# Splitting six of the experts' second weight tiles early, with GpSimd making their low parts

## The reference

```
gi = x @ W_ih + b_ih ; gh = h @ W_hh + b_hh            # 256 steps in sequence, batch 16, width 512
r = sigmoid(i_r + h_r) ; z = sigmoid(i_z + h_z)
n = tanh(i_n + r * h_n) ; h = (1 - z) * n + z * h
combine = two largest of softmax((h / |h|) @ router_w), normalised
out = x + sum over 8 experts e of combine[e] * (h @ Wa[e] @ Wb[e])      # rank 128
```

## Time and profile before

| what | value |
|---|---|
| median of 3 runs | 1009.75 us |
| the profiled execution | 1010.27 us |
| its span | 1008.5 us |
| PE busy | 977.9 us (97%) |
| DVE busy | 878.0 us (87%) |
| ACT busy | 689.5 us (68%) |
| POOL busy | 292.9 us (29%) |
| chain that ended last | PE 91%, DVE 4%, DMA 2%, ACT 1% |

### The profile page before, as it was taken

How to read it: one execution, slowest core, us unless ns; L and a number is a source line. 1 busy time by engine, 2 the same in 40 slices (tenths; PEclk the granted TensorE clock), 3 DMA queues, 4 the chain that set the end, 5 groups by cost and what they waited for, 6 DMA issues and landing times.

```text
span 1008.5 us, 60534 instructions
## 1 busy us (share of the span) xinstructions
PE 977.9 (97%) x28939; PEld 668.9 (66%) x20799; DVE 878.0 (87%) x3637; ACT 689.5 (68%) x2696; POOL 292.9 (29%) x755
## 2 busy tenths in 40 slices
PE   4789999999999999999999999999999999999997
PEld 2456666666667666677666666666676676676674
DVE  6889888888888888888888888888888888888887
ACT  6687766776766676666677676677666667666664
POOL 1032323332323332323332332332233332233223
PEclk9999999999999999999999999999999999999999
DMA  8321111111111111111111111101111101110000
GB/s 298 93 81 31 28 33 31 27 30 32 29 31 33 28 27 35 27 31 33 29 25 35 28 32 29 33 23 35 30 30 30 32 22 35 31 30 20 14 9 29
DMA packets 49360, 38.83 MB, mean 39 GB/s; under 512 B 34532, under 2 KB 38972, under 8 KB 49084
## 3 DMA queue, kind: packets, MB, share of 16 engines
q1 hardware_dynamic: 48236, 31.41, 11.5%
q10 hardware_dynamic: 848, 3.54, 1.0%
HBM read 18.94 MB, written 8.39 MB: 27 GB/s over the span
## 4 chain that ended last, share of the span: by engine, by line
PE 91%; DVE 4%; DMA 2%; ACT 1%; issue 1%; SPq 0%; POOL 0%; DVEq 0%; POOLq 0%
PE pairs L882 17%; PE ybank L882 12%; PE gates L962 11%; PE gates L967 11%; PE pairs L873 8%; PE ybank L873 5%; PE zbank L882 5%; PE zbank L873 5%; PE obank L882 5%; PE nbank L882 5%; PE obank L873 3%; PE nbank L873 3%; DMA whh<-in_L_cond_W_hh 1%; DVE tr L747 1%; PE ybank L999 1%; DMA xin<-in_x 1%
## 5 line engine op out<-in xcount | busy, mean ns | idle before, releaser
L882 PE MATMUL pairs<-wx,xs 128*32 128x384 f16 x4096 | 281.4, 328 | 0.2 <-DVE wx L727 0.2
L609 ACT ACTIVATE rr<-pre 128x64 f32<-128x64 f32 x256 | 65.7, 257 | 245.8 <-DVE pre L750 245.8
L882 PE MATMUL ybank<-hparts,wa 128*128 128x128 f16 x2048 | 194.1, 219 | 0.0
L882 PEld LDWEIGHTS ybank<-hparts,wa 128*128 128x128 f16 x2048 | 159.9, 98 | 29.8 <-issue 16.7
L873 PE MATMUL ybank<-hparts,wa 128*128 128x128 f16 x1024 | 178.3, 219 | 0.0
L463 POOL TENSOR_TENSOR y<-y 128x128 f16<-128x128 f32 x256 | 106.2, 435 | 247.3 <-ACT y L660 241.8
L873 PE MATMUL pairs<-wx,xs 128*32 128x384 f16 x2048 | 174.6, 327 | 0.0
L882 PEld LDWEIGHTS pairs<-wx,xs 128*32 128x32 f16 x4096 | 108.5, 97 | 95.0 <-issue 55.3
L962 PE MATMUL gates<-whh,st 128*32 128x256 f16 x4080 | 157.3, 273 | 12.7 <-DVE st L776 12.2
L962 PEld LDWEIGHTS gates<-whh,st 128*32 128x32 f16 x4080 | 107.4, 96 | 76.8 <-ACT gates L581 47.1
L967 PE MATMUL gates<-whh,hparts 128*32 128x256 f16 x4080 | 157.1, 273 | 0.0
(11 more groups left out here) (137 smaller groups left out, 1803.1 us busy)
## 6 DMA issues: line engine op xcount, KB each, us to landing
out<-outb SPq DMA_DIRECT2D x63, 128.0 KB
xin<-in_x SPq DMA_DIRECT2D x58, 128.0 KB
wih<-in_L_cond_W_ih ACTq DMA_DIRECT2D x4, 768.0 KB, 7.8
whh<-in_L_cond_W_hh SPq DMA_DIRECT2D x4, 768.0 KB, 11.8
wih<-in_L_ffn_Wb SPq DMA_DIRECT2D x8, 256.0 KB, 2.7
xs<-xh SPq DMA_TRANSPOSE x116, 3.1
wih<-in_L_ffn_Wa SPq DMA_DIRECT2D x4, 256.0 KB, 5.2
whh<-in_L_ffn_Wa SPq DMA_DIRECT2D x4, 256.0 KB, 2.9
```

Of the source, the lines that this page charges most:

```text
L609: nc.scalar.activation(rr[:, :], pre[:, RG, :, :].rearrange("p k b -> p (k b)"), ACT.Sigmoid, scale=1 / PROD_SCALE).then_inc(r_ready, 1)
L882: return nc.tensor.matmul(out, lhsT, rhs, start=start, stop=stop, skip_group_check=True)
```

## The change

Wb's tiles of experts 2 to 7 leave the list SPLITS (SHARED = 2 keeps experts 0 and 1 in it). Their high part is made by ACT in steps 4 to 9 (high_wb, WB_AT = 4), behind the late split of the same step. Their low part is made by POOL, at the head of its beside(n) in the same steps: the float32 tile is multiplied by 128 in place, then the high part is subtracted in two halves of 256 columns. PE waits on a new semaphore for them. The order of the late loads changes (the list LATE), and SP issues two a step from step 2 on, so that each of the six tiles is asked for two or three steps before its high part is due. DVE keeps the splits of wb 0 and 1 in steps 10 and 11 and has none after that.

```diff
+    SHARED, WB_AT = 2, 4
...
-        for e in range(NE):
+        for e in range(SHARED):
             split_wb(e)
...
+        LATE = [("wa", i) for i in range(K)]
+        for i in range(NE - SHARED):
+            LATE += [("wb", SHARED + i)] + ([("wa", K + i)] if i < K else [])
+        LATE += [("wb", i) for i in range(SHARED)]
...
+            def late_at(n):
+                return range(LEAD + n, LEAD + n + 1) if n < 2 else range(2 * n, 2 * n + 2)
...
-                if LEAD + n < 2 * K + NE:
-                    load_late(LEAD + n)
+                for late in late_at(n):
+                    if late < len(LATE):
+                        load_late(late)
...
+            def low_wb(e):
+                pool.wait_ge(wb_hi_ready, e - SHARED + 1)
+                nc.gpsimd.tensor_scalar(wb32[:, e, :], wb32[:, e, :], PART_SCALE, None, ALU.mult).then_inc(wb_scaled, 1)
+                pool.wait_ge(wb_scaled, e - SHARED + 1)
+                for half in range(2):
+                    cols = slice(half * D // 2, (half + 1) * D // 2)
+                    nc.gpsimd.tensor_tensor(wb[:, 1, e, cols], wb32[:, e, cols], wb[:, 0, e, cols], ALU.subtract
+                                            ).then_inc(wb_lo_ready, 1)
...
+                if 0 <= n - WB_AT < NE - SHARED:
+                    low_wb(SHARED + n - WB_AT)
...
+            def high_wb(e):
+                act.wait_ge(wb_loaded[e], 16)
+                nc.scalar.activation(wb[:, 0, e, :], wb32[:, e, :], ACT.Copy, scale=PART_SCALE).then_inc(wb_hi_ready, 1)
...
                 if 0 <= n < len(SPLITS) - N_GRU_SPLITS:
                     split_weights(N_GRU_SPLITS + n)
+                if 0 <= n - WB_AT < NE - SHARED:
+                    high_wb(SHARED + n - WB_AT)
...
                 if m in wb_split_at:
                     pe.wait_ge(weights_split, splits_before(wb_split_at[m]))
+                elif m < NE:
+                    pe.wait_ge(wb_lo_ready, 2 * (m - SHARED + 1))
```

More of the change, by code:

```diff
@@ L190, in gru_moe_kernel @@
         rw_loaded = sem("rw_loaded")
+        wb_hi_ready = sem("wb_hi_ready")
+        wb_lo_ready = sem("wb_lo_ready")
+        wb_scaled = sem("wb_scaled")
         hi_split = sem("hi_split")
@@ L338, in load_late @@
             def load_late(i):
-                if i < 2 * K:
-                    half, k = i // K, i % K
-                    if i == K // 2:
+                kind, of = LATE[i]
+                if kind == "wa":
+                    half, k = of // K, of % K
+                    if of == K // 2:
                         sp.wait_ge(weights_split, splits_before(N_GRU_SPLITS))
@@ L345, in load_late @@
                 else:
-                    e = i - 2 * K
-                    sp.dma_start(wb32[:, e, :], Wb[e]).then_inc(wb_loaded[e], 16)
+                    sp.dma_start(wb32[:, of, :], Wb[of]).then_inc(wb_loaded[of], 16)
+            def late_at(n):
+                return range(LEAD + n, LEAD + n + 1) if n < 2 else range(2 * n, 2 * n + 2)
             def beside(n):
```

## The result

| | kernel before | changed kernel |
|---|---|---|
| median, lowest to highest | 1009.80 us (1009.62 to 1010.88, 6 runs) | 1014.69 us (1013.81 to 1015.00, 6 runs) |
| profiled execution, its span | 1010.27 us, 1008.5 us | 1014.44 us, 1012.7 us |

The changed kernel is slower: the ratio is 1.0048, with a 95% interval of 1.0037 to 1.0058. That is 4.9 us more where 5.6 us were forecast, inside the range. The page's first part shows little of it: DVE and ACT hardly move, POOL has 13.8 us more, and PE has the same work in a longer span. It answers to the earlier trace rows.

A forecast was written before the change was run, and what follows sets the result against it. PE bounds the steady state, the recurrence chain steps 4 to 9, DVE's expert sum plus wb split steps 12 to 17. Terms -2.46 + 7.85 + 0.25 = +5.6 us on 1009.75 gave 1015.3 us, range 1009.0 to 1019.5.

The forecast's parts named there:

- The gain: Steps 12 to 17: six DVE low splits leave, steps fall from 25.06 to 22.60 us, 2.46 us saved.
- ACT: Early high copies stick out of ACT's idle time before the sigmoids of steps 7 and 9, costing about 0.65 us.
- POOL's meetings with the chain: Steps 5 to 10: POOL's reads hold off DVE's two-input chain instructions; 7.85 us together with ACT's 0.65.
- my upper row: Two-input POOL instruction of 1.35 us, the upper of two profile rows between which the scaling's 0.9 was taken.
- the walk: Tile-by-tile tracing of DVE's chain in steps 5 to 10 with POOL holds of 0.9, 0.53 and 0.53 us.
- The clock: Rival: TensorE's clock falls for two of the stretched steps, doubling state matmuls, 2.2 us, total 1017.5; chance 0.05.
- the forecast case: POOL's data phase holds DVE off in steps 5 to 10; total between 1011.8 and 1020.7 us, chance 0.60.
- What queues behind: POOL's router work comes some 3 us later around steps 9 to 11: 0.25 us, bounds 0 and 1.5.
- The sum: All terms over the whole kernel: -2.46 + 7.85 + 0.25 = +5.6 us, giving a median of 1015.3 us.
- that DVE isn't held off: Rival: DVE's chain in steps 5 to 10 goes first, only ACT's 0.65 is paid, total 1007.9; chance 0.15.
- That a meeting costs only 0.12: Rival: each POOL instruction meeting DVE's chain costs about 0.12 us, 2.2 in all, total 1010.1; chance 0.10.
- That the whole instruction holds: Rival: POOL holds DVE for its whole instruction, start-up included, 2.3 us more in all, total 1017.6; chance 0.10.

The follow-up runs named there:

- e6: The kernel before with DVE's low splits of tiles 2 to 7 left out and nothing moved: 1007.13 us against 1009.68.
- e1: The changed kernel without POOL's three instructions per tile (low parts zero), early ACT copies and load order kept: 1007.62 us against 1009.56 for the kernel before.
- e5: The changed kernel with six extra unread matmuls at the end of PE's work in steps 4 to 8 and 10: 1014.13 us.
- e2: The changed kernel with POOL's three instructions per tile replaced by memsets of about the same length that read nothing: 1009.26 us.
- e3: The changed kernel with POOL doing only the scaling of each tile, no subtractions: 1010.34 us.
- e4: The changed kernel with POOL doing only the two subtractions of each tile, no scaling: 1014.33 us.
- e8: The changed kernel with POOL's twelve subtractions alone, each after DVE's chain and POOL's router work, in steps 5 to 7 and 12 to 17: 1009.15 us.

## Why the prediction was right

The direction, the places and nearly the sum were right. The mechanism was the forecast one. That the sum came so near is luck: the term of POOL's meetings was too high by 1.9 us, and the clock and the displaced work brought about as much.

- *The gain*, 2.46 us: measured 2.40 (25.06 to 22.66), PE next to be late. e6 gives it alone, 2.21 in those steps and 2.55 in its median.
- *ACT*, 0.65 us, in steps 7 and 9: measured 0.67 by e1 against e6, 0.15 and 0.52 where 0.2 and 0.45 were forecast.
- *POOL's meetings with the chain*, 7.85 with ACT's part, so 7.2 without: this term was mis-sized. Steps 5 to 10 are 7.99 us longer. By the rows, the clock has 1.28 of that (twice 0.42 for the state matmuls and twice 0.22 for the z gate), by e5 1.38; ACT has 0.67. So 6.0 us are left. Of these about 0.7 are meetings of POOL's displaced work, for which the prediction had another term: in step 9 DVE's split lasts 1.23 us beside the squares and the next transpose starts 1.03 behind L996 in place of 0.67, and in step 10 L808 and L761 are 0.21 and 0.12 late. The new instructions' own meetings come to 5.3 us, 0.9 a tile and not 1.2. The step that failed is the scaling. I took its data time, 0.9, as its hold. It lasts longer than that, 1.49 us (more than the 1.35 of my upper row), and holds for 0.6. For the first tile the walk had 0.68 us for the scaling and 0.50 for both subtractions; measured are 0.22 and 0.83 (L786, then L805 and L808). So the subtractions were priced too low, and hid a part of the error.
- *The clock*: a rival with a chance of 0.05, at 2.2 us. It came, at 1.3 to 1.4 us, together with the forecast case and not instead of it. That is the second failed step: I set apart as a rival what follows from the forecast itself, for it was the stretched steps that let the clock fall.
- *What queues behind*, 0.25 with bounds 0 and 1.5, for new meetings and a wait: about 0.8, the 0.7 of meetings in steps 9 and 10 and 0.11 in step 11. e2 shows the 1.5 us that the wait costs when steps 9 and 10 don't hide it.
- *The sum*: -2.40 + 8.10 = +5.7 us in the steps, as forecast (+5.6). Median to median it is 4.9, and between the profiled executions 4.2. The difference lies outside of the steps that the change touches: the changed kernel's execution reached its transpose 0 at 26.29 us where that of before reached it at 27.07, and from transpose 18 to the last it took 891.75 us in place of 892.42. Over the eleven kernels the start lies anywhere between 26.2 and 27.2, so half a microsecond isn't told by such a comparison.
- *The rivals*: that DVE isn't held off fell with 0.57 to 0.71 us for instructions of 0.22. That a meeting costs only 0.12 fell too. That the whole instruction holds is wrong for the scaling (0.6 of 1.49) and nearly right for the subtraction.

## What to carry to other kernels

Before work is moved to an idle GpSimd, look at what VectorE does in the very microseconds in which it will run: two-input instructions of 0.22 us on a chain waited for GpSimd reads of 0.67 us, while memsets of the same length, and the same subtractions placed beside a split that isn't on the chain, cost the chain nothing. Ask as well what stands behind the new work in GpSimd's queue: waiting for it cost 1.5 us where nothing else hid it (e2), and what is pushed back can itself land on the chain (0.7 us in e3). And where a change stretches steps in which TensorE already waits, count the clock's fall with it and not beside it. A fall cost some 0.65 us here in steps in which TensorE waits, but 1.39 in a step in which it is full (e4's step 11).

## What the runs showed that I had not expected

- GpSimd's tensor_scalar of 128x512 float32 lasts 1.49 us, more than two subtractions of 256 columns (1.34 us), and yet holds VectorE's two-input instructions for its first 0.6 us only. Why, no run here tells.
- Steps that were only a microsecond longer let TensorE's clock fall. Before the first fall, at 48.24, TensorE had waited 1.88 us for the state and then done the sixteen matmuls of its first part; before the second, at 58.48, it had waited 1.78 us, done the sixteen and waited 0.53 more. Each fall lasted 3.41 us, and with six matmuls more in those waits (e5) there was none. The length of one wait doesn't tell it: in step 10 of the changed kernel TensorE waited 2.28 us and the clock stayed, in e4's step 10 it waited 2.27 and the clock fell 1.3 us after the wait had ended.
- When a VectorE split and a GpSimd subtraction start at the same time (51.60 in e8), VectorE's keeps its 0.65 us, and GpSimd's takes 1.19.
